# Sixteen-head attention on one NeuronCore: the end of a half goes from VectorE to ScalarE, VectorE and GpSimd

## The reference

```python
kv_input = jnp.concatenate([x, lat], axis=1)           # 7428 rows of width 128
k, v = jnp.split(kv_input @ Wkv, 2, axis=-1)
q = lat @ Wq
dots = jnp.einsum('bhid,bhjd->bhij', q, k) * scale
attn = jax.nn.softmax(dots, axis=-1)
out = jnp.einsum('bhij,bhjd->bhid', attn, v)           # 1024 x 64 for each head
return out.reshape(b, m, heads * dim_head) @ Wout
```

## Time and profile before

| | |
|---|---|
| median of three executions | 2393.45 us (2389.42 to 2393.76) |
| the profiled execution: its own time, and its span from first to last instruction | 2392.94 us, 2390.8 us |
| PE busy | 2252.1 us, 94% |
| DVE busy | 1865.2 us, 78% |
| ACT busy | 1670.9 us, 70% |
| POOL busy | 1858.8 us, 78% of the span; 1763.1 us of the 1918 between 123 and 2041 |
| granted TensorE clock from 123 to 2041 us | 1.00 |

### The profile page before, as it was taken

The page is one execution under the profiler, slowest core; times in us unless marked ns, Lnnn a source line. Parts: engine busy times, 40 slices in busy tenths (PEclk is TensorE's granted clock), DMA queues, the critical chain, the costliest instruction groups (busy, mean ns, idle before and its releaser), DMA issues. The chain is left out here.

```text
span 2390.8 us, 68504 instructions
## 1 busy us (share of the span) xinstructions
PE 2252.1 (94%) x27967; PEld 1469.2 (61%) x27967; DVE 1865.2 (78%) x3034; ACT 1670.9 (70%) x3028; POOL 1858.8 (78%) x1124
## 2 busy tenths in 40 slices
PE   2899999999999999999999999999999999679996
PEld 1366665666566656666666666656666666557885
DVE  8888888888888888888888888888887771448864
ACT  4677777777777777777777777777777777246662
POOL 1789999999999999999899999999999999240001
PEclk9999999999999999999999999999999999789998
DMA  2431314131413241324131413141314000340000
GB/s 90 121 83 44 95 63 123 41 98 63 123 41 93 67 118 46 93 67 118 41 98 60 121 46 93 62 122 43 97 49 115 2 2 2 129 86 2 2 2 13
DMA packets 124634, 165.68 MB, mean 69 GB/s; under 512 B 26392, under 2 KB 100192, under 8 KB 123872
## 3 DMA queue, kind: packets, MB, share of 16 engines
q1 hardware_dynamic: 122176, 157.53, 23.4%
q10 hardware_dynamic: 2144, 3.77, 0.5%
HBM read 99.28 MB, written 61.97 MB: 67 GB/s over the span
## 5 line engine op out<-in xcount | busy, mean ns | idle before, releaser
L635 POOL TENSOR_TENSOR att_prob_low<-att_prob 128x1024 f16<-128x1024 f32 x960 | 1765.5, 1865 | 161.1 <-PE all_banks L755 120.7
L912 ACT ACTIVATE att_prob<-all_banks 128x512 f32<-128x512 f32 x1888 | 1070.9, 591 | 386.7 <-PE all_banks L720 263.1
L1006 DVE TENSOR_REDUCE att_part<-all_banks 128x2 f32<-128x1024 f32 x581 | 695.6, 1216 | 79.6 <-PE all_banks L680 79.6
L741 PE MATMUL all_banks<-att_v,att_prob 128*128 128x129 f16 x5664 | 584.5, 221 | 2.4 <-ACT att_prob L912 0.3
L741 PEld LDWEIGHTS all_banks<-att_v,att_prob 128*128 128x128 bf16 x5664 | 414.2, 98 | 237.9 <-issue 10.7
L1010 DVE TENSOR_REDUCE att_part<-all_banks 128x1 f32<-128x512 f32 (+1 forms) x686 | 407.0, 636 | 114.8 <-PE all_banks L680 112.9
L755 PEld LDWEIGHTS all_banks<-att_v,att_prob_low 128*128 128x128 f16 x7552 | 328.5, 98 | 135.9 <-POOL att_prob_low L635 16.3
L701 PE MATMUL all_banks<-att_qc,att_kc 128*128 128x512 f16 x1056 | 401.7, 380 | 0.0
L702 PE MATMUL all_banks<-att_qd,att_kd 128*128 128x512 f16 x1056 | 401.5, 380 | 0.0
L755 PE MATMUL all_banks<-att_v,att_prob_low 128*128 128x65 f16 x7552 | 385.2, 194 | 11.8 <-POOL att_prob_low L635 11.7
L745 PE MATMUL all_banks<-att_v,att_prob 128*128 128x64 f16 x1888 | 371.5, 197 | 0.0
(11 more groups left out here) (313 smaller groups left out, 3043.4 us busy)
## 6 DMA issues: line engine op xcount, KB each, us to landing
v_all<-att_stage_v SPq DMA_DIRECT2D x98, 258.0 KB, 2.5
att_kc<-k_high SPq DMA_DIRECT2D x90, 232.0 KB, 3.9
att_v<-v_all SPq DMA_DIRECT2D x28, 483.8 KB
att_v<-v_all SPq DMA_DIRECT2D x28, 451.5 KB
k_high<-att_stage_h SPq DMA_DIRECT2D x98, 128.0 KB, 1.7
k_low<-att_stage_l SPq DMA_DIRECT2D x98, 128.0 KB, 1.9
att_kd<-k_low SPq DMA_DIRECT2D x45, 232.0 KB, 4.3
att_kc<-k_high SPq DMA_DIRECT2D x30, 232.5 KB, 4.4
```

The costliest lines, as they stand in the source:

```text
L635: pool.tensor_tensor(prob_low[g % NL][:, 0:w], p[:, 0:w], p.bitcast(BF16)[:, 1:2 * w:2], op=ALU.subtract).then_inc(low_split, 1)
L741: pe.matmul(O[:, q, :], w, v[:, e, t, :], start=first, stop=False, skip_group_check=True)
L912: act.activation(prob[g % NP][:, i * BANK:(i + 1) * BANK], S[n % 3], ACT.Exp, scale=SCALE)\
L1006: dve.tensor_reduce(parts[:, n:n + 2], pers.banks[:, 4 + 2 * pair:6 + 2 * pair, :], axis=AX.X, op=ALU.max)\
```

## The change

The reading of a half's sums moves out of DVE. ACT copies the 452 columns of the bank to an SBUF tensor (`raw`) in one instruction (`copy_sums`). It stands in ACT's queue in the first period of the next half, behind the first exponent. PE's `sums_free` waits for that copy instead of L1030 and L1031. DVE takes only the reciprocal, from the SBUF copy, and that at the end of the same period, behind maxima and seed (`invert_sums`). POOL joins the two products in `raw` (3x64 columns) and multiplies 4x64 columns by the reciprocals into `att`, ahead of its sixth unit (`NORM_AT` = 5) of the next half. The very last half is done behind the loops, in the same three steps. Semaphores for the new order take the place of the old ones.

```diff
--- before.py
+++ after.py
@@ -341,7 +341,9 @@
         nm = sc.sb("nm", [P, 2, HALF], F16)
         rden = sc.sb("rden", [P, 4])
         zeros = sc.sb("zeros", [P, P], F16)
-        rest = sc.sb("rest", [P, WIDE, DH])
+        SUM_COLS = WIDE * VCOLS + DH + 1
+        raw = sc.sb("raw", [P, 4 * VCOLS])
+        raw_o = raw[:, :].rearrange("p (j c) -> p j c", c=VCOLS)
         warm = sc.sb("warm", [1, 1])
         spare = sc.sb("spare", [P, 10])
         k_high = nc.dram_tensor("k_high", (INNER, KEYS), F16, kind="Internal").ap()
@@ -353,13 +355,14 @@
+        sums = pers.banks[:, :, :].rearrange("p b q -> p (b q)")[:, 0:SUM_COLS]
...
@@ -372,11 +375,12 @@
         parts = part[:, :, :].rearrange("p j c -> p (j c)")
         FIRST_LOW = [att[:, n, BANK:BANK + BANK // 2].bitcast(F16) for n in range(NF)]
 
-        EXP0, HIGH0, LOW0, SPLIT0, NORM0, OUT0 = 2, 3, 3, 3, 1, 32
+        EXP0, HIGH0, LOW0, SPLIT0, OUT0 = 2, 3, 3, 3, 32
         MEAN_PAIR = struct.unpack('f', struct.pack('2e', 1.0 / DH, 1.0 / DH))[0]
         SIDE = PAIRS + 1
         LAST = UNITS - 1
         SLOTS = TOKEN_TILES * K_CHUNKS
+        NORM_AT = 5
         PERIODS, OFFSET = UNITS // 2, 12
         HALF_TILES, HEAD_TILES = 2 * PAIRS + 1, 2 * (2 * PAIRS + 1)
         WINDOW = SLOTS // PERIODS
@@ -622,8 +626,24 @@
             for r in range(NR):
                 pool.memset(stage_v[r][:, :, :, :], 1.0).then_inc(v_ready, 1)
 
+            def normalize_half(b, h):
+
+                n = 2 * b + h + 1
+                o = raw_o[:, 0:WIDE, 0:DH]
+                pool.wait_ge(sums_copied, n)
+                pool.tensor_tensor(o, o, raw_o[:, 0:WIDE, DH + 1:VCOLS], op=ALU.add).then_inc(joined, 1)
+                pool.wait_ge(inverted, n)
+                pool.wait_ge(joined, n)
+                o = att[:, 4 * h:4 * h + 4, b * DH:(b + 1) * DH]
+                pool.tensor_tensor(o, raw_o[:, :, 0:DH], spread_columns(rden[:, :], DH), op=ALU.mult)\
+                    .then_inc(normalized, 1)
+
             def head(b):
                 for g in range(UNITS):
+                    if g == NORM_AT and b:
+                        normalize_half(b - 1, 1)
+                    elif g == SIDE + NORM_AT:
+                        normalize_half(b, 0)
                     pool.wait_ge(exp_done, EXP0 + place(b, g) + len(tiles(g)))
                     pool.wait_ge(low_done, LOW0 + b * UNITS + g - 2)
                     if g % SIDE == 0:
@@ -637,6 +657,7 @@
 
             for b in range(HEADS):
                 head(b)
+            normalize_half(HEADS - 1, 1)
 
         @block.tensor
         def _(pe):
@@ -726,9 +747,8 @@
                     pe.wait_ge(v_in[e], 16 * V_PIECES * turn)
                 elif g == 0:
                     pe.wait_ge(y_split, TASKS)
-                pe.wait_ge(normalized, NORM0 + 2 * b + g // SIDE)
                 if b or g:
-                    pe.wait_ge(rest_taken, 2 * b + g // SIDE)
+                    pe.wait_ge(sums_copied, 2 * b + g // SIDE)
 
             def apply_high(b, e, g, i):
                 pe.wait_ge(exp_done, EXP0 + place(b, g, i) + 1)
@@ -919,11 +939,22 @@
                 act.wait_ge(exp_done, EXP0 + n - 2)
                 act.activation(S[n % 3], nm[:, g // SIDE, :], ACT.Copy).then_inc(odd_seeded, 1)
 
+            def copy_sums(b, h):
+
+                act.wait_ge(low_done, LOW0 + b * UNITS + (h + 1) * SIDE)
+                if b or h:
+                    act.wait_ge(normalized, 2 * b + h)
+                act.activation(raw[:, 0:SUM_COLS], sums, ACT.Copy).then_inc(sums_copied, 1)
+
             def head(b, e, with_max, projecting, i):
                 for w in range(PERIODS):
                     last = 2 * w % SIDE == PAIRS - 1
                     n, after = place(b, 2 * w), place(b, 2 * w + 1) + len(tiles(2 * w + 1))
                     exp(n + 2)
+                    if w == 0 and b:
+                        copy_sums(b - 1, 1)
+                    elif 2 * w == SIDE:
+                        copy_sums(b, 0)
                     if not last:
                         exp(n + 3)
                     t = task_at(e, w) if projecting else None
@@ -972,6 +1003,7 @@
                 exp(n)
             for b in range(HEADS):
                 head(b, b % 2, b + 1 < HEADS, b // 2 + 1 < HEADS // 2, b // 2)
+            copy_sums(HEADS - 1, 1)
 
         @block.vector
         def _(dve):
@@ -1022,18 +1054,10 @@
                 dve.tensor_reduce(top[:, 4 * half:4 * half + 4], part[:, 4 * half:4 * half + 4, :], axis=AX.X, op=ALU.max)\
                    .then_inc(top_ready, 1)
 
-            def normalize_half(b, h):
-                dve.wait_ge(low_done, LOW0 + b * UNITS + (h + 1) * SIDE)
-                dve.reciprocal(rden[:, :], O[:, :, DH]).then_inc(inverted, 1)
-                dve.wait_ge(inverted, 2 * b + h + 1)
-                o = att[:, 4 * h:4 * h + 4, dyn(b * DH, DH)]
-                dve.tensor_tensor(o, O[:, :, 0:DH], spread_columns(rden[:, :], DH), op=ALU.mult).then_inc(normalized, 1)
-                dve.tensor_tensor(rest[:, :, :], O[:, 0:WIDE, DH + 1:VCOLS], spread_columns(rden[:, 0:WIDE], DH),
-                                  op=ALU.mult).then_inc(rest_taken, 1)
-                dve.wait_ge(normalized, NORM0 + 2 * b + h + 1)
-                dve.wait_ge(rest_taken, 2 * b + h + 1)
-                o = att[:, 4 * h:4 * h + WIDE, dyn(b * DH, DH)]
-                dve.tensor_tensor(o, o, rest[:, :, :], op=ALU.add).then_inc(rest_added, 1)
+            def invert_sums(b, h):
+
+                dve.wait_ge(sums_copied, 2 * b + h + 1)
+                dve.reciprocal(rden[:, :], raw_o[:, :, DH]).then_inc(inverted, 1)
 
             def head(b, e, with_max, projecting, i):
                 for w in range(PERIODS):
@@ -1049,11 +1073,12 @@
                     u = seeds_before(*next_period(b, w))
                     if u is not None and (w + 1 < PERIODS or with_max):
                         seed(place(b, 2 * w + 1) + len(tiles(2 * w + 1)) + 2, u)
-                    if 2 * w + 2 in (SIDE, UNITS):
-                        normalize_half(b, 2 * w // SIDE)
+                    if w == 0 and b:
+                        invert_sums(b - 1, 1)
+                    elif 2 * w == SIDE:
+                        invert_sums(b, 0)
 
             dve.memset(zeros[:, :], 0.0).then_inc(constants, 1)
-            dve.memset(spare[:, 1:2], 0.0).then_inc(normalized, NORM0)
             dve.memset(spare[:, 2:3], 0.0).then_inc(max_taken, 2)
             for r in range(NR):
                 dve.memset(spare[:, 4 + r:5 + r], 0.0).then_inc(kq_out[r], OUT0)
@@ -1071,6 +1096,7 @@
                     finish_max(0, 0)
             for b in range(HEADS):
                 head(b, b % 2, b + 1 < HEADS, b // 2 + 1 < HEADS // 2, b // 2)
+            invert_sums(HEADS - 1, 1)
 
 
 def stage_attention_out(nc, pers, A):
```

More of the change, by code:

```diff
@@ L360, in stage_attention @@
         (y_ready, y_copied, y_split, constants, filled, scored, exp_done, low_split, high_done, low_done,
-         max_scored, max_taken, top_ready, top_spread, top_placed, inverted, normalized, tail_ready,
-         v_ready, kd_ready, ident_ready, rest_taken, rest_added, nm_placed, even_seeded, odd_seeded) = (s[n] for n in names)
+         max_scored, max_taken, top_ready, top_spread, top_placed, inverted, joined, normalized, tail_ready,
+         v_ready, kd_ready, ident_ready, sums_copied, nm_placed, even_seeded, odd_seeded) = (s[n] for n in names)
         kq_out = [sc.sem(f"kq_out{n}") for n in range(NR)]
```

2 lines of the change are left out of this document (1 added, 1 removed).

## The result

The changed kernel took 2362.27 us (median of 4 runs, 2355.47 to 2376.12), the kernel before 2393.61 us (4 runs) beside it: a ratio of 0.9879, with a 95% interval of 0.984 to 0.9918. The profiled execution took 2361.5 us with a span of 2359.4 us, where 2360.5 was forecast.

The account below looks back on a forecast made before the run. PE bounds the attention heads, stalled at half boundaries by DVE's queue. Gains of 35.0 us at 27 boundaries less 2.6 (1.1 + 1.0 + 0.5) give net 32.4: 2392.94 to 2360.5 us, range 2356 to 2371.

Parts of the forecast that it names:

- (a): At half boundaries DVE no longer waits for the half's end; maxima start 1.33 us earlier, 0.1 us in hand.
- three losses: PE's losses at a boundary inside a head: 0.13 us at L741, 0.71 at L680, 0.38 at L710; all go.
- Rival 1: At boundaries the seed stays late, so 0.38 us at L710 stays 27 times; time 2371, chance 0.10.
- (b): L1036, DVE's 793 ns operation with both operands in SBUF, goes too; L1031 took 347 ns for as many columns.
- (c): ACT's new 452-column copy at each boundary takes 0.57 us, covered by ACT's 0.84 us of idle time.
- (d): DVE's one reciprocal behind the seed takes under 0.2 us, delaying second-period maxima that wait for PE in ordinary periods.
- (e): POOL's join and multiplication cost 1.37 us per half (1.2 to 2.6).
- The lateness allowed: POOL comes 0.9 us late at its sixth unit; covered, since it falls back 1.6 us in head 14 first.
- Rival 3: POOL's lateness passes to PE: its new work minus 0.5 us per half, for 31 halves; slower, chance 0.03.
- Heads 14 and 15: POOL is never idle there but at the boundary, so three halves lose 1.1 us and the last 1.0.
- The tail: Behind the last half nothing hides copy, join and multiplication: +0.5 us, between 0.3 and 0.7.
- Rivals 2, 4 and 5: POOL 2.6 us per half (0.07); stall only changes its name, 2390 to 2394 (0.03); larger gain, 2350 to 2355 (0.03).

Follow-up runs that it names:

- add_on_pool: The kernel before with only L1036, the sum with two SBUF operands, moved from DVE to POOL; 2364.16 us, ratio 0.9878 to the kernel before.
- recip_old_place: The changed kernel with DVE's reciprocal back where normalize_half stood, ahead of the new half's maxima, waiting for ACT's copy; 2371.24 us.
- pool_plus_2: The changed kernel with POOL's join and multiplication repeated twice more into an unused tile; 2410.59 us, ratio 1.0074 to the kernel before.
- pool_plus_1: The changed kernel with POOL's join and multiplication repeated once more into an unused tile; 2374.54 us, ratio 0.9931 to the kernel before.
- after_again: The changed kernel run again without an edit, as the measure for runs beside it; 2359.69 us, ratio 0.9852 to the kernel before.
- last_three_on_dve: The changed kernel with join and multiplication of the last three halves on DVE instead of POOL; 2356.88 us, ratio 0.9851 to the kernel before.
- dve_old_place: The changed kernel with reciprocal, join and multiplication all on DVE at the old place, ahead of the maxima; 2505.21 us, ratio 1.0463 to the kernel before.

## Why the prediction was right, point by point

- **(a), DVE's queue**: right. All three losses went at the boundary read here, and the waits at L680 and L710 are gone. The term was 1.22 us inside a head and 1.38 between heads, 35.0 in all. From the end of a half's last L755 or L775 to the first L710 or L731 of the next, the first 27 boundaries took 35.0 us less in sum, as added up. But the halves took 32.5 less, not 35.0, so 2.5 came back. The 0.1 us in hand was less: ACT's seed, which I had not followed, is done last now, and costs 0.08 at L734, 27 times 0.08 = 2.2 us. Rival 1 is this mechanism at a fifth of its price.
- **(b), L1036**: I named it in one sentence as going along with the rest. add_on_pool shows that, taken off alone, it brings the larger part: 25 of 32 us. The forecast didn't need the division, but a reader who had to choose one edit would have been misled by my order.
- **(c), ACT's copy**: 0.57 taken, 547 ns measured, hidden everywhere but for ACT's seed.
- **(d), the reciprocal**: 169 ns, hidden. recip_old_place shows that its place was worth at least its length: 0.22 us per half.
- **(e), POOL**: 1.37 taken, 1.25 measured (527 and 617 ns). The Trainium skill's factor ("GPSIMD Engine Reference", "4.1 Engine selection"), about 2 times slower than DVE, would have given an estimate of 1.6; the trace gives less. The rule itself, that such work belongs on VectorE, was the wrong way round here: on DVE the two took 3.0 us (1069 and 1948 ns on average) beside POOL at the old place. The lateness allowed was put at 1.6 us with 0.9 used, so 0.7 to spare; measured, 0.9. The second half of the argument, that POOL makes its lateness good within the half, is true of the change (above) but did not decide: in pool_plus_2 the halves with time to make it good lost like the others. Rival 3 had the edge at 0.5 us of new work; pool_plus_1 would then have been 31 x 1.87 = 58 us slower over the halves and was 10.8.
- **Heads 14 and 15**: right in sign, too high in size (0.3 us for the four halves, where I had 1.1 + 1.0), and one term was misread. The three full halves took 56.73, 56.73 and 56.73 us after 56.61, 56.61 and 56.68: 0.3 in all for the 1.1. The last took 56.58 after 56.54, so nothing for the 1.0. But the idle 1.25 us ahead of its third unit, of which I let 0.35 shrink and took the rest for a fixed part of the boundary, went wholly. It was the clock. Stretches of the kernel before at that place (busy times, then the granted clock):

```profile
1980.00:1982.00 2.00, 1.22 (x6) 0.32 (x6) 0.87 (x3) 0.19 (x2) 1.83 (x2) 0.69 0.00 0
1982.00:1984.00 2.00, 1.90 (x15) 1.38 (x16) 1.41 (x2) 0.54 (x1) 2.00 (x2) 0.50 0.03 8
```

and of the changed kernel, with POOL's row behind it:

```profile
1950.00:1954.00 4.00, 3.00 (x39) 1.82 (x35) 0.77 (x2) 2.35 (x5) 3.83 (x3) 1.00 0.02 4
```

```profile
1951.14 9.41 POOL L655 TENSOR_TENSOR att_prob_low<-att_prob 128x1024 f16<-128x1024 f32 x5 [0.17 <-POOL att_prob_low L655]
```

In after_again the dip was there (0.58 over the same four us), and with it 0.67 us of idle time at this unit; its last half took 57.42 us. With a dip in both kernels the last half is thus 57.42 - 56.54 = 0.9 us longer, close to the 1.0 of the sum. That it came out at nothing is luck of the profiled execution, in which the changed kernel had no dip.

- **The tail**: PE's first L1101 stood 2039.33 - 2037.6 = 1.7 us after the mark before; now its counterpart comes 2010.20 - 2007.93 = 2.3 after: +0.6, where +0.5 was forecast.

The mis-sized terms nearly cancel: 2.5 us less gain in the first 27 halves, 1.8 less loss in the last four, half of it by the dip. That, and spreads of some 2 us ahead of and behind the halves that happened to cancel too, is why the profiled execution came out 1.0 us and the median 1.8 us above the 2360.5, closer than the terms deserved. Rivals 2, 4 and 5 did not come: POOL's pieces cost 1.25 us, no wait of a few tenths took the old ones' place, and no further gain was there.

## What to carry to other kernels

Read at each wait what stands in the queue behind it: an instruction that waits early for a late event makes hurried work late, and moving it behind that work can bring as much as taking it away. Before an operation with two SBUF operands is given to DVE beside a busy POOL, look for another of the kind in the trace, and count for each with up to a whole instruction of POOL's (1.9 us here) instead of its own length. An engine with a busy share of 90% and more can still take work, as long as its lateness stays below what those who wait for it have in hand (here near 2.2 us per half); repeat the new work once and twice to see how far that edge is, and don't take the idle time left in a whole half for it.

## What the runs showed of the hardware

**DVE can be held for many instructions of POOL, not one.** In last_three_on_dve, POOL's run first:

```profile
1899.74 50.12 POOL L659 TENSOR_TENSOR att_prob_low<-att_prob 128x1024 f16<-128x1024 f32 x27 [1.04 <-ACT att_prob L936]
...
1941.17 8.90 DVE L1070 TENSOR_TENSOR att_raw<-att_raw 128x192 f32<-128x192 f32 x1
...
2007.64 0.33 DVE L1070 TENSOR_TENSOR att_raw<-att_raw 128x192 f32<-128x192 f32 x1
```

The same join takes 0.33 us once POOL is idle, and 8.90 us while POOL reads SBUF without a break; it ends at 1950.07, just after POOL's run does (1899.74 + 50.12 = 1949.86), though of the 27 units in that run, a new one every 1.86 us, four ended in between. This happened once. In dve_old_place the join ended 0.21 us and the multiplication 0.28 us behind the end of a single unit at every boundary (1.07 and 1.95 us on average), and a second join in last_three_on_dve, at 1953.28, got in after one unit, with 0.07 us between that unit and the next. The Trainium skill, "SBUF — State Buffer", "SBUF: two separate sides", says that of a DVE operation with two SBUF inputs and a GpSimd operation that reads SBUF, whichever starts first has the shared ports for its whole instruction and the other is blocked. dve_old_place agrees with that; the 8.90 us show that the wait can outlast several instructions, when POOL starts each unit without a gap.

**A stall of 2.3 us can be followed by half the clock for a while.** Stretches of dve_old_place around a stall at 184.3 to 186.6 (behind the busy times the granted clock, as a share of the full):

```profile
183.00:187.00 4.00, 1.72 (x16) 0.89 (x14) 3.90 (x5) 1.86 (x4) 3.57 (x2) 0.94 0.00 0
187.00:191.00 4.00, 3.67 (x20) 1.66 (x19) 3.38 (x5) 1.09 (x2) 0.22 (x1) 0.50 0.00 0
191.00:195.00 4.00, 4.00 (x38) 2.24 (x36) 1.46 (x3) 2.37 (x4) 1.72 (x1) 0.71 0.19 63
195.00:199.00 4.00, 4.00 (x51) 2.54 (x51) 3.54 (x5) 3.05 (x6) 3.36 (x3) 1.00 0.04 11
```

0.50 is 1.2 of 2.4 GHz. PE finishes 20 matmuls in four us, and 51 in the last four of these rows, and between 187 and 195 us the clock gives 4 x 0.50 + 4 x 0.29 = 3.2 us less than its full share, at most what PE loses. This is one of the two longest dips of these halves: the half is 65.4 us instead of the 60.9 of the kernel before, of which the stall accounts for 2.2. Dips followed 28 of the 30 stalls; the others of the first 27 halves are half as long and made their halves 1.1 to 1.6 us longer. The stall at 252.13 of the same kernel was followed by none (1.00 in the next stretches). Dips also stood at boundaries in the late heads of most executions, the kernel before among them (above), where PE had idled for 1.00 and 0.79 us shortly before; the changed kernel had the same two idle times (1949.82 and 1951.02) and no dip. What decides whether one comes is open, and so is the spread of some us in the stages behind attention.
